# A fused attention and feed-forward kernel on one core: start-up transfers put in another order with semaphores of their own, ScalarE's long copies moved, 22 dummy products

## What is computed

```
xn  = layernorm(x)
h   = tanh(xn @ W1.T + b1);  s = h @ w2 + b2
e   = exp(s - max(s));  ctx = cumsum(e * xn) / cumsum(e)      # over a sequence
att = tanh(concat(ctx, xn) @ Wc.T + bc)
ffn = (silu(xn @ (wg/127).T) * (xn @ (wu/127).T)) @ (wd/127).T  # wg, wu, wd: int32, 768 hidden
out = x + att + ffn
```

## Time and profile before

| | |
|---|---|
| runs | 417.49 us median (417.26 to 418.5) |
| profiled execution: its own time, its span | 415.07 us, 413.3 us |
| TensorE products busy | 402.4 us, 97% of the span, 2857 products |
| VectorE, ScalarE, GpSimd busy | 75%, 61%, 40% of the span |
| mean granted TensorE clock | 0.996 of full speed |

### The profile page before, as it was taken

How to read it: one execution, slowest core, us unless ns; L and a number is a source line. 1 busy time by engine, 2 the same in 40 slices (tenths; PEclk the granted TensorE clock), 3 DMA queues, 4 the chain that set the end, 5 groups by cost and what they waited for, 6 DMA issues and landing times.

```text
span 413.3 us, 7888 instructions
## 1 busy us (share of the span) xinstructions
PE 402.4 (97%) x2857; PEld 282.2 (68%) x2857; DVE 311.8 (75%) x664; ACT 251.1 (61%) x465; POOL 165.0 (40%) x228
## 2 busy tenths in 40 slices
PE   8779999999999999999999999999999999999996
PEld 3436767676758768667868677686766677686765
DVE  5698999999789998778685866788667578655351
ACT  3888586858498684873883855536445453536350
POOL 0250220131306996728070520788618367402000
PEclk9899999999999999999999999999999999999999
DMA  8997000000003252131100011422221220101001
GB/s 257 338 349 227 2 3 0 2 1 2 0 19 90 51 142 67 50 78 43 61 27 25 28 51 32 127 74 80 103 76 50 79 87 16 52 2 52 27 26 59
DMA packets 24431, 29.50 MB, mean 71 GB/s; under 512 B 1216, under 2 KB 19648, under 8 KB 24384
## 3 DMA queue, kind: packets, MB, share of 16 engines
q1 hardware_dynamic: 24384, 28.91, 22.9%
...
## 4 chain that ended last, share of the span: by engine, by line
PE 69%; DVE 18%; issue 5%; SPq 2%; DMA 2%; ACT 2%; POOL 2%; DVEq 0%; ACTq 0%; POOLq 0%
PE bank L578 32%; PE bank L603 29%; PE bank L623 7%; DVE stats L791 3%; DVE bank L928 3%; DVE ex L951 2%; DVE wide L933 2%; DMA tri<-in_tri 2%; DVE bank L913 2%; PE bank L571 1%; DVE xres L937 1%; DVE xt L903 1%; DVE mv L795 1%; SPq L1097 1%; POOL wide L1039 1%
## 5 line engine op out<-in xcount | busy, mean ns | idle before, releaser
L603 PE MATMUL bank<-xt,narrow 128*128 128x512 f16 x768 | 179.7, 381 | 0.9 <-DVE xt L903 0.7
L603 PEld LDWEIGHTS bank<-xt,narrow 128*128 128x128 f16 x768 | 75.1, 98 | 76.7 <-issue 1.7
L578 PE MATMUL bank<-narrow,wide 128*128 128x256 f16 x792 | 96.3, 273 | 0.0
L578 PE MATMUL bank<-narrow,xt 128*128 128x256 f16 x768 | 92.9, 274 | 3.0 <-ACT bank L698 3.0
L578 PEld LDWEIGHTS bank<-narrow,xt 128*128 128x128 f16 x768 | 75.2, 98 | 19.5 <-issue 3.4
L578 PEld LDWEIGHTS bank<-narrow,wide 128*128 128x128 f16 x792 | 77.5, 98 | 9.4
L729 ACT ACTIVATE sg<-bank 128x512 f32<-128x512 f32 x96 | 57.3, 597 | 40.4 <-PE bank L603 40.2
L736 ACT ACTIVATE wide<-bank 128x512 f16<-128x512 f32 x90 | 53.8, 598 | 44.1 <-DVE bank L928 43.4
L928 DVE SCALAR_TENSOR_TENSOR bank<-bank,sg 128x512 f32<-128x512 f32 x96 | 66.3, 695 | 16.7 <-PE bank L603 16.0
L1039 POOL TENSOR_TENSOR wide<-ex,wide 128x512 f16<-128x512 f32 x32 | 39.2, 1243 | 92.5 <-ACT wide L749 92.5
L933 DVE TENSOR_TENSOR wide<-bank,wide 128x512 f16<-128x512 f32 x90 | 60.7, 678 | 16.8 <-ACT wide L736 16.0
...
## 6 DMA issues: line engine op xcount, KB each, us to landing
...
```

The source lines that it names most:

```text
L578: return pe.matmul(dst, lhs, rhs, start=False, stop=stop, skip_group_check=True)
L603: mm = pe.matmul(b[:, :], pg.up(which, k, j), pg.xn(sx, k, tok), start=n == 0, stop=n == len(todo) - 1)
```

## The change

The order of the transfers is now x of block 0, W1, the identity, b1, wg, wu, w2 with b2, x of block 1, wd, x of block 2, Wc, bc, tri, then the rest of x. `bias` is sent in two parts, and b1, bc, w2b2 and tri have a semaphore each; `Cs` waits for bc, `M2` for tri. `Kg` has to come after `Wgh`, and `Wgh` after the second high half `Xh` of block 0. The numbers from which the planner works (`BEGIN`, `SENT`, the landing of x, the due times of the turns and of `B`) are new. There are 22 dummy products instead of 25, and the last gives a semaphore `p_warm`, for which each `Ss` waits.

```diff
-BEGIN = {TE: 9.6, SE: 2.5, VE: 10.1, PO: 1.0, SY: 31.0}
+BEGIN = {TE: 9.1, SE: 2.5, VE: 9.9, PO: 1.0, SY: 33.0}
...
-        turn = 2.0 + 3.6 * (i - 1) if i else -1
+        turn = 2.5 + 3.55 * (i - 1) if i else -1
...
     if kind == "Kg":
-        return [(("Kg", 0, 0), 0), (("Ss", 0, 1), 0)] if x else []
-    follows = {"Wgh": ["W1h"], "Wch": ["Wgh"], "W1l": ["W1h"], "Wcl": ["W1l", "Wch"], "Wdh": ["Wuh"],
+        return [(("Kg", 0, 0) if x else ("Wgh", 0, 0), 0)]
+    follows = {"Wgh": ["W1h", "Xh1"], "Wch": ["Wgh"], "W1l": ["W1h"], "Wcl": ["W1l", "Wch"], "Wdh": ["Wuh"],
...
-        WARM = 25
+        WARM = 22
...
+                pe.wait_ge(s_tri, 16)
...
             elif kind == "Ss":
-                if (i, n) == (0, 0):
-                    act.wait_ge(s_bias, 16)
+                act.wait_ge(s_b1, 16)
+                act.wait_ge(p_warm, 1)
...
             elif kind == "Cs":
+                act.wait_ge(s_bc, 16)
...
-                    dve.wait_ge(s_cst, 16 * N_CONST)
+                    dve.wait_ge(s_w2, 16)
...
+            sp.dma_start(w1_32, halves(w1)).then_inc(s_w1, 16)
+            sp.dma_start(ident[:, :], ident_in).then_inc(s_ident, 16)
+            sp.dma_start(bias[:, 0:D], biases[0:D].partition_broadcast(P)).then_inc(s_b1, 16)
             sp.dma_start(half(wg32.bitcast(I32)), halves(wg)).then_inc(s_wg, 16)
-            sp.dma_start(ident[:, :], ident_in).then_inc(s_ident, 16)
-            sp.dma_start(w1_32, halves(w1)).then_inc(s_w1, 16)
             sp.dma_start(half(wu32.bitcast(I32)), halves(wu)).then_inc(s_wu, 16)
-            sp.dma_start(bias[:, :], biases.partition_broadcast(P)).then_inc(s_bias, 16)
+            sp.dma_start(w2b2[:, :], w2b2_in.partition_broadcast(P)).then_inc(s_w2, 16)
+            load_x(1)
+            sp.dma_start(wd32.bitcast(I32).rearrange("p (k n) -> p k n", k=KH), halves(wd)).then_inc(s_wd, 16)
+            load_x(2)
             sp.dma_start(wc_32, halves(wc)).then_inc(s_wc, 16)
-            sp.dma_start(wd32.bitcast(I32).rearrange("p (k n) -> p k n", k=KH), halves(wd)).then_inc(s_wd, 16)
-            sp.dma_start(w2b2[:, :], w2b2_in.partition_broadcast(P)).then_inc(s_cst, 16)
-            load_x(1)
-            sp.dma_start(tri[:, :], tri_in).then_inc(s_cst, 16)
-            for i in range(2, NBLK):
+            sp.dma_start(bias[:, D:], biases[D:2 * D].partition_broadcast(P)).then_inc(s_bc, 16)
+            sp.dma_start(tri[:, :], tri_in).then_inc(s_tri, 16)
+            for i in range(3, NBLK):
                 load_x(i)
...
-                pe.matmul(bank[n % BANKS][:, :], warm[:, 0:P], warm[:, 0:BLK], start=True, stop=True)
+                mm = pe.matmul(bank[n % BANKS][:, :], warm[:, 0:P], warm[:, 0:BLK], start=True, stop=True)
+            mm.then_inc(p_warm, 1)
```

More of the change, by code:

```diff
@@ L74 @@
 LAST = NBLK - 1
-BEGIN = {TE: 9.6, SE: 2.5, VE: 10.1, PO: 1.0, SY: 31.0}
-SENT = {"Kg": 6.8, "Wgh": 6.8, "W1h": 8.2, "K1": 8.2, "Ku": 9.7, "Wuh": 9.7, "Kc": 11.8, "Wch": 11.8, "Wdh": 13.4,
-        "Kd": 13.4, "Ke": 13.4}
+BEGIN = {TE: 9.1, SE: 2.5, VE: 9.9, PO: 1.0, SY: 33.0}
+SENT = {"W1h": 6.2, "K1": 6.2, "Kg": 8.8, "Wgh": 8.8, "Ku": 11.2, "Wuh": 11.2, "Sv": 11.7, "Kd": 15.4, "Ke": 15.4,
+        "Wdh": 15.4, "Kc": 18.6, "Wch": 18.6}
 ONCE = ("B", "R", "T")
@@ L143, in due_times @@
             for n, i in enumerate(blocks):
-                due["B", i, 0], due["B", i, 1] = first - 13.0 + 2.0 * n, first - 12.0 + 2.0 * n
+                due["B", i, 0], due["B", i, 1] = first - 10.0 + 2.0 * n, first - 9.0 + 2.0 * n
             due["R", g, 0], due["T", g, 0] = first - 8.5, first - 8.4
@@ L193, in needs @@
     if kind == "Kg":
-        return [(("Kg", 0, 0), 0), (("Ss", 0, 1), 0)] if x else []
-    follows = {"Wgh": ["W1h"], "Wch": ["Wgh"], "W1l": ["W1h"], "Wcl": ["W1l", "Wch"], "Wdh": ["Wuh"],
+        return [(("Kg", 0, 0) if x else ("Wgh", 0, 0), 0)]
+    follows = {"Wgh": ["W1h", "Xh1"], "Wch": ["Wgh"], "W1l": ["W1h"], "Wcl": ["W1l", "Wch"], "Wdh": ["Wuh"],
                "Kp": ["Kf"], "Fl": ["Kp"], "BrT": ["Fl"], "BrS": ["Fl"], "BrV": ["Fl"], "BrG": ["Fl", "Wdh"], "BrY": ["Fl"]}
     if kind in follows:
-        return [((other, 0, 0), 0) for other in follows[kind]]
+        return [(("Xh", 0, 1) if other == "Xh1" else (other, 0, 0), 0) for other in follows[kind]]
     if kind == "Kf":
@@ L290, in __init__ @@
         self.order = []
-        self.times = {0.0, *BEGIN.values(), *SENT.values(), *(15.0 + 1.6 * i for i in range(NBLK))}
+        self.times = {0.0, *BEGIN.values(), *SENT.values(), 9.2, 9.9}
         while any(self.todo.values()):
@@ L453, in block_kernel @@
             sem, ("a_ok", "a_xn", "a_x", "a_ss", "a_s", "a_sg", "a_h", "a_c", "a_cs", "a_y", "a_e", "a_w"))
-        p_ok, p_x, p_s, p_g, p_u, p_d, p_y, p_m = map(
-            sem, ("p_ok", "p_x", "p_s", "p_g", "p_u", "p_d", "p_y", "p_m"))
+        p_warm, p_ok, p_x, p_s, p_g, p_u, p_d, p_y, p_m = map(
+            sem, ("p_warm", "p_ok", "p_x", "p_s", "p_g", "p_u", "p_d", "p_y", "p_m"))
         g_rs, g_x, g_ex, g_clo, g_w = map(sem, ("g_rs", "g_x", "g_ex", "g_clo", "g_w"))
-        N_CONST = 2
         M_MAX, M_NEG, M_DEN, M_RECIP, M_T = 3, 4, 6, 10, 11
```

8 lines of the change are left out of this document (4 added, 4 removed).

## The result

The changed kernel is slower. Its median is 421.53 us (419.44 to 425.08, 12 runs) against 415.97 us for the kernel before in the same session (415.58 to 418.5, 12 runs): the ratio is 1.012, with a 95% interval from 1.0091 to 1.0149. The prediction had 413.1 us, with a range from 411.0 to 415.7, and gave slower a chance of 0.05: it said 4.35 us less, and these medians are 5.6 us apart the other way. The profiled execution of the changed kernel took 423.21 us, its span is 421.4 us; before, these were 415.07 and 413.3.

The account below looks back on a forecast made before the run. TensorE's chain of products bounds the kernel, with gains only in the first 30 us. 4.45 us less, minus 0.1 for the branch, gives 4.35 off 417.49: 413.1 us, range 411.0 to 415.7.

Parts of the forecast that it names:

- What moves the other way: Whole kernel: possible losses from Kc, weight copies, added waits and VectorE's load, counted as nothing; the sum allows 0.1 for the branch.
- the prediction's own signs of being wrong: Among them: clock at 0.50 after the turns or after 25 us, or over 1 us of TensorE waits after 30 us.
- The line of sizes: Start: landing times read from the old order's bytes against time, 216 KiB per us at first, then 379, then 339.
- First S: Block 0 on TensorE: starts at 11.15 instead of 13.46, released by VectorE's low half, 2.3 us earlier.
- Second S: Start, on TensorE: begins at 14.2 against 18.17, 3.97 us earlier.
- None waits: The next eight Gg and Gu, 15.5 to 22.4: their banks come free in time, so no waits.
- T of block 1: GpSimd's root steps for block 1, 3.85 us long, end at 21.1, so Ln starts then instead of at 25.55.
- The gap before the second turn: TensorE idle 2.2 us, 22.9 to 25.1, before block 1's second turn, where it sat 1.71 before.
- The rival that it falls in the new gap: Clock falls in the 2.2 us gap before block 1's second turn, costing 1.7 us: 414.8 us; chance 0.12.
- the clock's term: Start: with a gap of only 0.75 us, no clock fall near 14 us, saving 1.7 us; bounds 0 to 1.7.
- the one with the late transfers: Transfers or VectorE take most back, S starting at 12.5: 1.5 to 3 us remain, 414.5 to 416; chance 0.10.
- The slower rival: Kc on VectorE, ahead of block 1's Xl, waits for a late Wc and holds the whole chain; chance 0.05.

Follow-up runs that it names:

- run 12: The changed kernel with the scan of block 3, pair 0, planned behind the low half Xl of block 11, pair 0: 416.26 us, ratio 0.998 to the kernel before.
- run 3: The changed kernel with the start's transfers sent in the old order, b1 and bc still apart: 421.83 us, ratio 1.0103 to the kernel before.
- run 4: The changed kernel with b1's transfer reading as many bytes of x instead of one broadcast row: 420.88 us, ratio 1.0075 to the kernel before.
- run 11: The changed kernel with the scan of block 3, pair 1, planned behind both low halves Xl of block 11: 417.06 us, ratio 1.0009 to the kernel before.
- run 1: The changed kernel with the last root (R 9 on VectorE, T 9 on GpSimd) planned behind N of block 3: 416.7 us, ratio 0.9972 to the kernel before.
- run 9: The kernel before with T 9 put ahead of Cl of block 2 and N of block 3, its place in the changed kernel: 416.02 us, ratio 0.9974.
- run 5: The changed kernel with only T 9 on GpSimd planned behind N of block 3, R 9 staying early: 417.38 us, ratio 0.9991 to the kernel before.
- run 6: The changed kernel with the last root late and the traced landing times in the planner's table: 414.93 us, ratio 0.9952 to the kernel before.
- run 10: The changed kernel with late last root and traced landings in the planner, repeated in another session: 414.47 us, ratio 0.9932 to the kernel before.
- run 7: As run 6, but with wg sent ahead of W1 and the planner's table fitted to that: 415.4 us, ratio 0.9966 to the kernel before.
- run 2: The kernel before with T 9 planned ahead of N of block 3, though behind Cl of block 2: 416.09 us, ratio 0.9975.
- run 8: The kernel before with only a semaphore each for w2b2 and tri, all orders old: 415.3 us, ratio 0.9974.

## Why the prediction was wrong

**The ledger.** Run 12 has the changed kernel's TensorE list, and its profiled execution kept full clock throughout, with a span of 412.4 us, 9.0 less than the changed kernel's. So the two timelines can be laid side by side, here run 12:

```profile
28.25 0.66 PE L569 MATMUL bank<-ident,xnat 128*128 128x128 f32 x4 [2.16 <-DVE xt L903]
...
39.90 1.47 PE L621 MATMUL bank<-narrow,ex 128*128 128x256 f16 x12
...
174.88 1.04 PE L569 MATMUL bank<-ident,xnat 128*128 128x128 f32 x8
...
178.38 1.89 PE L601 MATMUL bank<-xt,narrow 128*128 128x512 f16 x8
...
182.72 1.47 PE L576 MATMUL bank<-narrow,wide 128*128 128x256 f16 x12
```

The row at 174.88 stands at 179.73 in the changed kernel, that at 178.38 at 185.60 and that at 182.72 at 191.63. At the first D the changed kernel is 41.77 - 39.90 = 1.9 us behind, 1.7 of it from the slow stretch after the second turn (28.45 to 41.77 against 28.25 to 39.90). Up to 179.73, the waits near 163 and 172 make 4.85 - 1.87 = 3.0 more (idle 2.41, and some 0.17 a wait on top, since a product behind a wait starts later than one behind a product), the one at 185.60 makes 7.22 - 4.85 = 2.4, and the slow stretch behind it 8.91 - 7.22 = 1.7. Together 8.9 of 9.0. Most of the wait near 163, 0.72 us for a bias, is a matter of the execution: with the same lists up to there, runs 3 and 4 have 0.21 and 0.19 of it and run 11 none. The kernel before lies 0.9 behind run 12, its own wait of 0.70 at 179.27.

**The step that failed** is the paragraph "What moves the other way", which puts all that lies between the start and TensorE's step 214 at nothing. It asks whether the weight copies, the added waits and VectorE's load between 40 and 110 us take the gain back. Of the stretch from 110 us to step 214 it says nothing, neither a term nor a reason. Its last sentence, "From step 214 the lists agree, so nothing is due there", came true: step 214 runs near 252 us in the kernel before (`M3` behind it starts at 252.81) and near 260 in the changed one, and the loss stands ahead of it. The windows of the changed kernel (TensorE's busy time is the first number behind the comma):

```profile
150.00:190.00 40.00, 35.38 (x251) 24.84 (x249) 33.75 (x52) 24.82 (x48) 26.70 (x31) 0.96 0.29 81
...
240.00:300.00 60.00, 60.00 (x440) 42.99 (x439) 44.27 (x72) 34.14 (x62) 31.77 (x22) 1.00 0.24 71
300.00:360.00 60.00, 60.00 (x434) 42.27 (x433) 42.94 (x51) 29.36 (x54) 35.00 (x24) 1.00 0.20 63
```

TensorE works 35.38 of the 40 us from 150 to 190, where it had 39.30, and all of the time behind. The three long waits there, at 162.91, 171.59 and 185.60, are its steps 140, 145 and 156 (counted from 0, as step 214 is), and from step 131 to 181 its two lists agree as well. So a list that agrees still waits when those that feed it don't agree, and the comparison that was made for TensorE alone had to be made for all engines: in the planner's listing of GpSimd `T` 9 stands behind both `N` of block 3 before and ahead of them after, and the rows of order ahead of the prediction stop at the start. The price of this stretch, waits and slow clock, is 3.0 + 2.4 - 0.9 + 1.7 = 6.2 us in the profiled executions, against nothing in the prediction; the ratios of the changed kernel and run 1 give 6.2 too, the medians 4.8. Two of the prediction's own signs of being wrong came, a clock of 0.50 after 25 us and more than 1 us of TensorE's waits after 30 us (5.1 us), but neither had a place or a price there.

**The mechanism in the middle** is shown by runs 9, 11 and 12: not the place of `T` 9 alone (0.9974 in run 9) and not GpSimd's delay alone (1.84 us of wait in run 11 too), but the two together with a VectorE list in which both scans of block 3 stand ahead of the low halves of block 11. The kernel before has them ahead as well, and there it costs nothing, since `N` is early. Either repair is enough: `T` 9 late (0.9972, 0.9991) or the scan late (1.0009, 0.998). That covers the wait near 172. The one near 185 is 0.70 us before, 1.59 in run 11 and none in run 12; what share of the 2.21 is due to the same chain stays open.

Which number of the planner did it can be read from the lists it makes, without a run: with the old due times of the turns, 2.0 + 3.6 per block, or the old landings of x, and all else new, `T` 9 comes behind `N` 3 again. That these variants would be fast wasn't tried.

**The landings** were the second error. "W1 6.0" was right (the copy starts at 5.46), but b1 was put at 6.9 and used at 9.63, wg at 9.5 and 11.56, wu at 11.6 and 13.53, x of block 1 at 13.5 and 16.48, wd at 15.75 and 18.78. The line of sizes was read off the old order as if only bytes counted. In the new order the queue moved fewer of them: from 5 to 8 us, after in the first row and before in the second,

```profile
5.00:8.00 3.00, 3.00 (x14) 1.27 (x13) 2.48 (x16) 0.63 (x1) 0.00 (x0) 1.00 0.62 146
...
5.00:8.00 3.00, 3.00 (x10) 1.09 (x9) 2.51 (x16) 0.00 (x0) 0.00 (x0) 1.00 1.01 345
```

146 against 345 GB/s, with the DMA engines busy 0.62 of the time. That is 0.6 MB behind after three microseconds, or 1.7 us at the 354 GB/s of the three that follow. Run 4 shows that the broadcast of b1 makes wg and wu at most 0.7 us of that late; why the rate sinks to 251 GB/s even there stays open. For the 3 us of x and wd there is more (x of block 1 is issued at 4.73 and lands 11.7 us later, and from 11 to 14 us the rate is 304 GB/s against 357), and its cause is open too.

**The forecast by its steps.** Dummies and turns: 9.2 foreseen, 9.03 measured. First S: 11.15 foreseen, 11.62 measured: the releaser is the one that I named, the time is outside the 0.3 us that I allowed, by b1's landing. Gu of block 0 at 13.3: wrong, 15.16 after 0.94 us of waiting for `Wuh`, by the late wu. Second S: 14.2 foreseen, 16.02 measured, since a gate product waits ahead of it. "None waits" of the next eight: wrong, 0.90 us behind `Sv`. T of block 1: 21.1 foreseen, 24.2 measured, by wd. The gap before the second turn: 2.2 foreseen, 2.16 measured, but at 28.45 and not 25.1. So the -4.0 us of the turn became -0.67, and the -4.45 of the S behind it -1.12 (28.94 against 30.06); most of that goes back to the late landings above.

That the clock would not fall near 14 held in this execution and is no rule: in run 5, with the same lists up to there, it is 0.50 from 11.5 to 14.5, after a gap of 1.24 us. The rival that it falls in the new gap came true: 1.7 us, as priced. In runs 5, 11 and 12, with the same lists up to there, it kept up, so it is a matter of the execution and no fixed cost. The page "TensorE: Matmul & The Clock Gate" of the Trainium skill, in its section on oscillation, has bursts of products whose waits for data, longer than the gaps here, are each followed by a fall that is paid anew. The trace agrees twice in the changed kernel (2.16 and 2.21 us idle, 0.50 after both) and not in run 12, where 2.16 us idle is followed by full speed.

**What the start is worth.** In run 12, at full clock, the attention product near 177.1 comes at the time it has before, 177.07 against 177.09. The gain that reaches D, 0.1 us and one step of 0.86 done earlier, is given back in two waits, 0.15 at 60.20 and 0.34 at 77.24, which cost some 0.17 each on top from start to start. And that gain is the clock's: the kernel before has its slow stretch of 1.67 us ahead of D and run 12 has none. Apart from it the new start is 0.7 us longer than the old one (1.67 - 0.86 - 0.09), since it begins 0.6 us earlier and takes 1.3 us more from the turns to D, with waits of 5.9 us there against 4.7. So of the sum's 4.45 us only the clock's term of 1.67 was there, and only where no later gap makes the clock fall.

Of the rivals, the one with the late transfers (0.10) named the right cause for the start, though not that nothing would be left. With the table fitted to the real landings (runs 6 and 10, 0.5 and 0.7%) more stays. Run 1 has the same late root and the guessed table and stands at 0.28%; its interval touches both, so that it is the table is likely and not shown. Run 7's 0.3% is no more than that of runs 2, 8 and 9. The slower rival, Kc waiting for Wc, had the right sign by the wrong mechanism: Kc starts at 23.61 without a wait.
